# Where VectorE's expert-choice tasks stand among the steps of the attention stage: spread evenly, or by a running sum of TensorE's work

## The chip, the cores and the metric

The kernel runs on one core of a Trainium2 chip. The metric is the device time of one execution in microseconds (us); the time given for a kernel is the median of its runs. TensorE does the matrix products, VectorE reductions, comparisons and copies, ScalarE activations and copies out of the accumulator banks, GpSimd elementwise work; SyncE issues the DMAs. Each engine runs its own program in order, and they meet through semaphores.

## The reference, cut to what matters

```python
def reference(x, ctx_1024, ...):                       # x, ctx: 4 x 512 x 256
    x = x + xattn(layernorm(x), ctx_1024, ctx_1024)    # 16 heads of 16, softmax(q k^T / 4) v, Wo
    x = x + ffn(layernorm(x))
def ffn(x):                                            # product-key experts, 8 heads
    q = (rmsnorm(x) @ wq).reshape(B, T, 8, 2, 128)
    sim = einsum('bthpd,hkpd->pbthk', q, keys)         # 2 x 64 scores for each head and token
    s1, i1 = top_k(sim[0], 16);  s2, i2 = top_k(sim[1], 16)
    scores = s1[..., :, None] + s2[..., None, :]       # 256 candidates
    final_scores, pk = top_k(scores, 16)               # 16 experts of 4096
    hidden = gelu(x_norm . expert_down[idx]) * relu(final_scores)
    return sum(hidden * expert_up[idx])
```

The 2048 tokens make 16 tiles of 128. The choice of experts (both `top_k` levels) is VectorE's work.

## The kernel before

The program has two stages. In the attention stage, groups `g` = 0 to 20 (`SLOTS`) run one after the other; a group is four heads of one batch element, and has 16 steps `i`. "Step 11.9" is step 9 of group 11. At each step:

- TensorE runs the `event`s that the table `plan` gives for the step, then a turned-score product of group g - 2 (`turned_scores`), then the score product of group g (`scores`), and at every fourth step (1, 5, 9, 13) the four value products (`values`). Events: `xT`, `cT`, `proj`, `v`, `aT`, `o`, `yT` (layer norms, projections and outputs of a batch element), `max`, `oT` (each group), `down`, `wqT`, `kyT`, `wqk` (weights), `sim` (the key scores of a tile, fp32, steps 1 and 2 of even groups from 8 on), `tok` (the chosen numbers turned, step 6).
- VectorE reduces the score bank of the step to its row maxima (`tensor_reduce`, L1201), then does its other attention work if the step has any (`max_parts` at step 0, `normalise` at step 4, `first_norm` at 3 and `first_norm_apply` at 8 of groups 0, 4, 8, and in groups 6, 10, 14, 18 `residual` at steps 12 and 14 and `second_norm` at 13 and 15), and then the tasks of the choice that the table `choice` gives for the step.

TensorE may be three score products ahead of VectorE: `scores` for step n waits for the reduction of step n - 3 (`pe.wait_ge(s_max, n - 2)`, three banks). All waits are in each engine's program order, so a TensorE that waits in `scores` also holds back its events.

The choice for a tile is 17 tasks: eight `search` (a head each: top 16 of twice 64 scores, L1080 to L1092), four `choose` (two heads each, among 50 candidates a head, L1099 to L1111), one `keys` (L1120 to L1126), and four `extract` (two heads each, L1133 to L1140; the last is followed by `decode`, L1149 to L1158). Six tiles (`NA`) are chosen in this stage: tile t begins at group 8 + 2t, and its tasks stand at steps 5 to 31 counted from there, placed evenly by `spread`. The other ten tiles are chosen in the second stage.

GpSimd's program in this stage is in order too. In group g it makes, for the tile that begins there, `candidates` of heads 0 to 3 (after four searches; `choose` 0 waits for them); in the next group `candidates` of heads 4 to 7 (`choose` 2 waits for them), `expert_numbers` (`keys` waits for them), in groups 1, 5, 9 then the four `split_projection`, in groups 6, 10, 14, 18 `second_scale` twice, and last `weight_parts` after the tile's `decode`. `second_scale` is seven small instructions between VectorE's `residual` (its last instruction is L1049) and `second_norm` (L1060):

```python
                if ends:
                    candidates(tile, 1)
                    expert_numbers(tile)
                ...
                if r == 2 and b >= 1:
                    second_scale(2 * (b - 1))
                    second_scale(2 * (b - 1) + 1)
```

SyncE issues, in group g: the relay of the maxima of group g - 1, twelve loads of the score operands of group g + 1, in groups 1, 5, 9 `store_parts` four times (each after a GpSimd split), and in odd groups from 7 on the load of the next tile's input for `sim` (`load_sim_input`, L527). The second stage begins when every engine has reached `phase`; it needs the choices of tiles 0 to 5.

Of the kernel before, what the change touches and what calls it, by code (L numbers as in the profile page):

```python
# [19 lines left out]
HG = 4  # L20
NG = B * H // HG
# [45 lines left out]
def build(nc, x, ctx_in, Wq, bq, Wk, bk, Wv, bv, Wo, bo, norm_w, wq, keys, down, up, out):  # L67
    ctx = ExitStack()
    with ctx:
        def sem(name):  # L70
# [16 lines left out]
        wqk = mem.take(KD * HP * NK).rearrange("p (k n) -> p k n", k=KD)  # L87
# [4 lines left out]
        sim = mem.take(HP * NK)  # L92
# [16 lines left out]
        tok = mem.take(5 * P // 2, BF16).rearrange("p (c n) -> p c n", c=5)  # L109
# [8 lines left out]
        xT = mem.take(KD * S).rearrange("p (k t) -> p k t", k=KD)  # L118
        cT = mem.take(KD * S).rearrange("p (k t) -> p k t", k=KD)
        proj = [mem.take(S) for _ in range(2)]  # L120
# [6 lines left out]
        oT = [mem.take(S) for _ in range(2)]  # L127
        attn = mem.take(TB * D).rearrange("p (t d) -> p t d", t=TB)
        aT = mem.take(KD * S).rearrange("p (k t) -> p k t", k=KD)
# [27 lines left out]
        wqT = mem.take(2 * KD * P).rearrange("p (c k f) -> p c k f", c=2, k=KD)  # L157
        kyT = mem.take(2 * NK).rearrange("p (c n) -> p c n", c=2)
# [10 lines left out]
              for _ in range(2)]  # L169
# [10 lines left out]
        SLOTS = NG + 5  # L180
        NA = 6
        TASKS = ([("search", h) for h in range(FH)] +  [("choose", s) for s in range(4)] +
                 [("keys", 0)] + [("extract", s) for s in range(4)])

        def spread(n_tiles, first, steps):

            n = n_tiles * len(TASKS)
            return [(first + t * (steps - first) // n, t // len(TASKS), *TASKS[t % len(TASKS)]) for t in range(n)]

        def choice_start(tile):  # L190
            return 2 * HG + 2 * tile

        choice = {}
        for _t in range(NA):
            for _s, _, _kind, _i in spread(1, 5, 32):
                choice.setdefault((choice_start(_t) + _s // 16, _s % 16), []).append((_t, _kind, _i))
        before = [(0, "xT", (0, 0)), (0, "xT", (0, 1)), (0, "cT", (0, 0)), (0, "cT", (0, 1)), (0, "proj", (0, 0)),
                  (0, "proj", (0, 1)), (0, "proj", (0, 2)), (0, "proj", (0, 3)), (0, "v", (0, 0)), (0, "v", (0, 1))]
        plan = []
        for g in range(SLOTS):  # L200
            b, r = g // HG, g % HG
            ev = []
            if 1 <= g <= NG:
                ev.append((3, "max", g - 1))
            if 3 <= g < NG + 3:
                ev.append((4, "oT", g - 3))
            if r == 0 and b + 1 < B:
                ev += [(11, "xT", (b + 1, 0)), (12, "xT", (b + 1, 1)), (13, "cT", (b + 1, 0)), (14, "cT", (b + 1, 1))]
            if r == 1 and b + 1 < B:
                ev += [(2 + 3 * n, "proj", (b + 1, n)) for n in range(4)]  # L210
            if r == 2 and b + 1 < B:
                ev += [(3, "v", (b + 1, 0)), (5, "v", (b + 1, 1))]
            if r == 2 and b >= 1:
                ev += [(8, "aT", (b - 1, 0)), (9, "aT", (b - 1, 1)), (12, "o", (b - 1, 0)), (14, "o", (b - 1, 1))]
            if r == 3 and b >= 1:
                ev += [(6, "yT", (b - 1, 0)), (8, "yT", (b - 1, 1))]
            if g % 2 == 0 and g >= choice_start(0):
                tile = (g - choice_start(0)) // 2
                if tile < NA:
                    ev += [(1, "sim", (tile, 0)), (2, "sim", (tile, 1))]  # L220
                if 1 <= tile <= NA:
                    ev.append((6, "tok", tile - 1))
            if g < JL // 2:
                ev.append((7, "down", g))
            if g < HP // 2:
                ev += [(9, "wqT", g), (10, "kyT", g), (15, "wqk", g)]
            plan.append(sorted(ev, key=lambda e: e[0]))
        order = {(n, i): e for e, (_, n, i) in enumerate(before + [e for s in plan for e in s])}

        misc_full = [sem("misc_full0"), sem("misc_full1")]  # L230
# [1331 lines left out]
```

## Time and profile before

| | before |
|---|---|
| median of 3 runs | 1234.25 us (1229.91 to 1236.24) |
| the profiled execution | 1233.31 us, span 1231.5 us |
| TensorE matmuls | 1062.0 us busy, 86% of the span |
| VectorE | 948.9 us busy, 77% |
| GpSimd | 615.3 us busy, 50% |
| ScalarE | 393.8 us busy, 32% |
| mean granted TensorE clock | 0.922 |

The attention stage takes roughly the first 520 us; the part with choices in it is 214 to 516 us. Shares over the whole span mix the two stages, so the sections below go by stretches. Times of rows are us from the span's start.

### The profile page before, as it was taken

The page shows a single profiled execution, that of the slowest core. Times are in us where ns is not written, and L with a number is a line of the kernel's source. Part 1 is how long each engine was busy: PE and PEld are TensorE (multiplying, and loading weights), DVE is VectorE, ACT ScalarE, POOL GpSimd, SP SyncE. Part 2 cuts the span into 40 slices and gives each one's busy share as a digit, 9 for nine tenths or more (in the row PEclk, how much of TensorE's full clock was granted, in tenths as well). Part 3 has the DMA queues.
Part 4 walks back from the last instruction along what each step waited for, and adds up shares of the span by engine and source line. Part 5 has one row for each costly group of instructions (what it writes and reads, how often), then busy time and mean ns, then how long its engine had stood idle before and what let it go on. Part 6 is the DMA issues. An engine that isn't in the chain of part 4 may idle for free.

```text
span 1231.5 us, 28859 instructions
## 1 busy us (share of the span) xinstructions
PE 1062.0 (86%) x10152; PEld 731.2 (59%) x10152; DVE 948.9 (77%) x4836; ACT 393.8 (32%) x717; POOL 615.3 (50%) x772
## 2 busy tenths in 40 slices
PE   4899987878878777057998999999999999999998
PEld 2444443323212323036787887888878888888887
DVE  4757554968998999669899999998989989953310
ACT  2257544433444353013222222222222222222211
POOL 6320410332210313225777787877877696877511
PEclk9799998888787798556999999999999999999999
DMA  5344313221221110180010000000100010000000
GB/s 166 116 149 143 106 44 121 66 72 49 83 73 47 34 43 6 47 318 3 1 30 16 16 26 17 20 25 11 39 12 25 2 34 16 26 15 24 2 18 9
DMA packets 59924, 63.76 MB, mean 52 GB/s; under 512 B 6882, under 2 KB 56164, under 8 KB 59268
## 3 DMA queue, kind: packets, MB, share of 16 engines
q1 hardware_dynamic: 59780, 61.90, 15.7%
q8 instruction: 83, 1.36, 0.5%
q14 instruction: 61, 0.50, 0.1%
HBM read 42.21 MB, written 19.66 MB: 50 GB/s over the span
## 4 chain that ended last, share of the span: by engine, by line
PE 53%; DVE 27%; POOL 7%; issue 6%; DMA 3%; SPq 2%; ACT 2%; DVEq 0%; POOLq 0%; ACTq 0%
PE bank L1282 50%; DVE mem L1201 4%; PE bank L1285 3%; POOL mem L792 2%; DVE mem L1137 2%; DVE mem L1238 2%; DVE mem L1084 2%; DVE mem L1083 2%; SPq L492 2%; DVE mem L1088 1%; DVE mem L1133 1%; DVE mem L1140 1%; DVE mem L1080 1%; DVE mem L1092 1%; DVE mem L1120 1%
## 5 line engine op out<-in xcount | busy, mean ns | idle before, releaser
L1282 PE MATMUL bank<-mem 128*128 128x32 bf16 (+5 forms) x9672 | 1012.4, 276 | 100.2 <-DVE mem L1201 35.7
L1282 PEld LDWEIGHTS bank<-mem 128*128 128x128 bf16 (+3 forms) x9672 | 679.0, 123 | 382.9 <-issue 175.8
L792 POOL TENSOR_TENSOR mem<-mem 128x1536 bf16<-128x1536 bf16 x118 | 325.7, 2761 | 156.2 <-DVE mem L1235 151.9
L1201 DVE TENSOR_REDUCE mem<-bank 128x1 f32<-128x512 f32 x256 | 167.9, 682 | 87.1 <-PE bank L1282 86.8
L908 ACT ACTIVATE mem<-bank 128x512 f32<-128x512 f32 x256 | 149.0, 601 | 207.9 <-PE bank L1282 207.0
L1238 DVE TENSOR_TENSOR mem<-mem,bank 128x2048 bf16<-128x2048 bf16 x128 | 155.4, 1214 | 0.0
L1285 PE MATMUL bank<-mem 128*128 128x128 f32 (+3 forms) x480 | 75.9, 290 | 66.0 <-POOL mem L704 25.0
L1285 PEld LDWEIGHTS bank<-mem 128*128 128x128 f32 (+3 forms) x480 | 54.9, 142 | 113.8 <-issue 71.0
L799 POOL TENSOR_TENSOR mem<-mem 128x512 f32<-128x512 f32 x64 | 83.5, 1305 | 50.5 <-ACT mem L947 50.5
L958 ACT COPY mem<-bank 128x512 f32<-128x512 f32 x128 | 74.9, 585 | 104.8 <-PE bank L1282 104.8
L673 POOL TENSOR_TENSOR mem<-mem 128x32 f32<-128x32 f32 (+5 forms) x224 | 45.7, 242 | 117.7 <-DVE mem L1092 117.7
L1235 DVE TENSOR_TENSOR mem<-mem,bank 128x512 bf16<-128x512 bf16 x128 | 52.6, 411 | 66.0 <-PE bank L1282 56.6
L949 ACT ACTIVATE bank<-bank 128x512 f32<-128x512 f32 x64 | 37.2, 582 | 167.2 <-PE bank L1282 167.2
L947 ACT ACTIVATE mem<-bank 128x512 f32<-128x512 f32 x64 | 38.3, 598 | 163.2 <-PE bank L1282 163.2
L1252 DVE TENSOR_TENSOR mem<-bank,mem 128x512 f32<-128x512 f32 x64 | 43.8, 685 | 47.0 <-ACT bank L949 39.0
L694 POOL TENSOR_TENSOR mem<-mem 128x128 f32<-128x128 f32 x16 | 6.9, 431 | 98.9 <-DVE mem L1154 98.9
L1083 DVE FIND_INDEX8 mem<-mem 128x8 uint32<-128x64 f32 x256 | 52.9, 219 | 0.0
L1084 DVE MATCH_REPLACE8 mem<-mem 128x64 f32<-128x64 f32 x256 | 51.5, 209 | 0.0
L1137 DVE MATCH_REPLACE8 mem<-mem 128x50 f32<-128x50 f32 x256 | 46.9, 194 | 0.0
L1088 DVE MAX8 mem<-mem 128x8 f32<-128x64 f32 x256 | 44.2, 214 | 0.0
L1080 DVE MAX8 mem<-mem 128x8 f32<-128x64 f32 x256 | 43.5, 211 | 0.0
L708 POOL TENSOR_SCALAR mem<-mem 128x4 f32<-128x4 f32 x4 | 0.9, 234 | 78.2 <-DVE mem L997 78.2
(103 smaller groups left out, 764.1 us busy)
## 6 DMA issues: line engine op xcount, KB each, us to landing
mem<-parts_d SPq DMA_DIRECT2D x192, 64.0 KB, 2.3
parts_d<-mem SPq DMA_DIRECT2D x16, 384.0 KB, 2.6
mem<-in_L_ffn_expert_down SPq DMA_DIRECT2D x16, 256.0 KB, 3.0
downT_d<-mem SPq DMA_DIRECT2D x16, 256.0 KB, 3.2
mem<-downT_d SPq DMA_DIRECT2D x4, 1024.0 KB, 8.5
mem<-in_L_ffn_expert_up SPq DMA_DIRECT2D x4, 1024.0 KB, 16.7
tok_d<-mem SPq DMA_DIRECT2D x16, 160.0 KB, 1.8
mem<-tok_d SPq DMA_DIRECT2D x16, 160.0 KB, 2.4
```

Source lines behind the costliest of these rows:

```text
L792: nc.gpsimd.tensor_tensor(ow[q % 2], i0, i1, ALU.mult).then_inc(ow_rdy, 1)
L799: nc.gpsimd.tensor_tensor(gm[q % 4], gm[q % 4], coef[par][:, 2 * q:2 * q + 2, :], ALU.mult)\
L908: nc.scalar.activation(p_sb[quad % 3][:, hh, :], psum[3 + n % 2][:, :], ACT.Exp, scale=DK ** -0.5)\
L958: nc.scalar.copy(coef[1 - par][:, :, q * TK:(q + 1) * TK], src).then_inc(c_ev, 1)
L1083: steps.count(nc.vector.max_index(i[:, h, c, 0:8], s[:, h, c, 0:8], src[c]))
L1084: cut = [steps.count(nc.vector.match_replace(left[c], s[:, h, c, 0:8], src[c], GONE)) for c in range(2)]
L1088: top.append(steps.count(nc.vector.max(s[:, h, c, 8:16], left[c])))
L1137: b.append(steps.count(nc.vector.match_replace(k[:, h, :], o[:, h, 0:8], k[:, h, :], 0.0)))
L1201: nc.vector.tensor_reduce(nmx[g % 2][:, i % TB, i // TB:i // TB + 1], psum[n % 3][:, :], AX.X, ALU.max, negate=True).then_inc(s_max, 1)
L1238: nc.vector.tensor_tensor(oh[q % 2], high.to_broadcast([P, TP, P, PAIR]), numbers.unsqueeze(1).to_broadcast([P, TP, P, PAIR]), ALU.is_equa ...
L1282: return nc.tensor.matmul(o, l, r, start=first, stop=last)
L1285: return nc.tensor.transpose(o, i, ident)
```

## The change

The table `choice` is made in another way; nothing else differs. Each step gets a number, `room`: 3, and 4 for each unit of TensorE's events at the step after it (`PE_WORK`), less 4 for each unit of VectorE's own work at the step (`DVE_WORK`), and at least 1. The 17 tasks of a tile are put where the running sum of these numbers over steps 5 to 31 passes each seventeenth of its total.

```diff
-        choice = {}
-        for _t in range(NA):
-            for _s, _, _kind, _i in spread(1, 5, 32):
-                choice.setdefault((choice_start(_t) + _s // 16, _s % 16), []).append((_t, _kind, _i))
...
+        PE_WORK = {"proj": 4, "v": 5, "o": 5, "sim": 4, "xT": 2, "cT": 2, "aT": 2, "yT": 2, "oT": 2, "down": 2, "wqT": 2,
+                   "max": 1, "tok": 1, "kyT": 1, "wqk": 1}
+        DVE_WORK = {(0, 3): 4, (0, 8): 4, (2, 12): 4, (2, 13): 2, (2, 14): 4, (2, 15): 2}
+
+        def room(g, i):
+
+            own = DVE_WORK.get((g % HG, i), 0) if g < NG + HG else 0
+            after = plan[g + (i + 1) // 16] if g + (i + 1) // 16 < SLOTS else []
+            return max(1, 3 + 4 * sum(PE_WORK[name] for at, name, _ in after if at == (i + 1) % 16) - 4 * own)
+
+        choice = {}
+        for _t in range(NA):
+            _at = [(choice_start(_t) + s // 16, s % 16) for s in range(5, 32)]
+            _sum = list(itertools.accumulate(room(g, i) for g, i in _at))
+            for _n, (_kind, _i) in enumerate(TASKS):
+                _s = next(j for j, total in enumerate(_sum) if total * len(TASKS) > _n * _sum[-1])
+                choice.setdefault(_at[_s], []).append((_t, _kind, _i))
```

Worked out by the two rules, the tasks stand at these steps (s search, c choose, k keys, e extract; the group's number before the point):

```
tile 1 before: s 10.5 .6 .8 .9 .11 .12 .14 11.0 | c 11.1 .3 .4 .6 | k 11.8 | e 11.9 .11 .12 .14
tile 1 now:    s 10.5 .6 .7 .8 .9 .11 .11 .13   | c 10.13 11.1 .3 .3 | k 11.5 | e 11.6 .7 .9 .12
tile 3:        as tile 1, four groups later, before and now
tile 0 now:    s 8.5 .6 .10 .11 .12 .13 9.0 .1  | c 9.2 .3 .4 .5 | k 9.6 | e 9.7 .9 .10 .12
tile 2 now:    s 12.5 .5 .6 .7 .10 .12 .14 13.0 | c 13.2 .3 .3 .5 | k 13.6 | e 13.7 .9 .11 .13
tile 4 now:    s 16.5 .5 .7 .9 .11 .13 .15 17.0 | c 17.2 .3 .3 .5 | k 17.7 | e 17.8 .10 .12 .14
tile 5 now:    s 18.5 .6 .7 .8 .9 .11 .11 .11   | c 18.13 .13 19.1 .4 | k 19.5 | e 19.7 .7 .10 .13
before, every tile has the pattern of tile 1 before, counted from its own first group
```

The instructions of VectorE show this in two places. The first is the second half of group 10, around the first `residual` (L1040, BN_STATS and BN_AGGR) and its `second_norm` (L1060); L1080 to L1092 are one search, L1201 is the reduction of a step. Before, from step 10.12 on:

```order
L1201 TENSOR_REDUCE mem<-bank 128x1
L1040 TENSOR_TENSOR mem<-bank,mem 128x512
L1044 BN_STATS mem<-mem 128x6 x2
L1049 BN_AGGR mem<-mem 128x2 x2
L1080 MAX mem<-mem 128x8 x2
L1083 MAX_INDEX mem<-mem 128x8 x2
L1084 MATCH_REPLACE mem<-mem 128x64 x2
L1088 MAX mem<-mem 128x8 x2
L1090 MAX_INDEX mem<-mem 128x8
L1092 MAX_INDEX mem<-mem 128x8
L1201 TENSOR_REDUCE mem<-bank 128x1
L1060 TENSOR_SCALAR mem<-mem 128x256 x2
```

Now (all line numbers are 15 higher), the same steps; L1095 is the first line of a search:

```order
L1216 TENSOR_REDUCE mem<-bank 128x1
L1055 TENSOR_TENSOR mem<-bank,mem 128x512
L1059 BN_STATS mem<-mem 128x6 x2
L1064 BN_AGGR mem<-mem 128x2 x2
L1216 TENSOR_REDUCE mem<-bank 128x1
L1075 TENSOR_SCALAR mem<-mem 128x256 x2
L1095 MAX mem<-mem 128x8 x2
```

The search that stood between BN_AGGR and the `second_norm` is gone from there; the same holds for the pair at steps 14 and 15.

The second place is the end of group 11, where the tile's last task (extract and decode, L1133 to L1158) stands. Before, from the reduction of step 12 on:

```order
L1201 TENSOR_REDUCE mem<-bank 128x1
L1133 MAX mem<-mem 128x8 x4
L1137 MATCH_REPLACE mem<-mem 128x50 x4
L1140 MAX mem<-mem 128x8 x4
L1201 TENSOR_REDUCE mem<-bank 128x1 x2
L1133 MAX mem<-mem 128x8 x4
L1137 MATCH_REPLACE mem<-mem 128x50 x4
L1140 MAX mem<-mem 128x8 x4
L1149 TENSOR_SCALAR mem<-mem 128x128
```

Now, from the reductions of steps 10 to 12 on to those of steps 13 to 15:

```order
L1216 TENSOR_REDUCE mem<-bank 128x1 x3
L1148 MAX mem<-mem 128x8 x4
L1152 MATCH_REPLACE mem<-mem 128x50 x4
L1155 MAX mem<-mem 128x8 x4
L1164 TENSOR_SCALAR mem<-mem 128x128
L1166 TENSOR_SCALAR mem<-mem 128x128
L1167 TENSOR_SCALAR mem<-mem 128x128
L1169 SCALAR_TENSOR_TENSOR mem<-mem 128x128
L1172 CAST mem<-mem 128x128
L1173 CAST mem<-mem 128x128
L1216 TENSOR_REDUCE mem<-bank 128x1 x3
```

The last extract and the decode moved from behind the reduction of step 14 to behind that of step 12.

## Rows read from the trace of the kernel before

**Rows 1.** Stretches: us, busy us of PE, PEld, DVE, ACT, POOL, clock, DMA.

```profile
262.80:281.00 18.20, 16.16 (x61) 6.79 (x63) 4.06 (x8) 5.03 (x11) 1.20 (x4) 0.88 0.06 17
281.00:334.10 53.10, 42.35 (x186) 15.86 (x187) 51.03 (x304) 22.12 (x43) 11.84 (x40) 0.81 0.23 71
334.10:340.20 6.10, 5.52 (x28) 1.99 (x28) 3.27 (x8) 3.57 (x7) 0.71 (x2) 1.00 0.01 1
...
394.00:446.00 52.00, 42.37 (x184) 15.93 (x180) 50.01 (x301) 21.27 (x40) 10.94 (x38) 0.84 0.17 52
```

**Rows 2.** VectorE's waits, 281 to 334: us, times, longest.

```profile
DVE mem L1201 <- PE bank L1282: 2.4, 1, 2.4
DVE mem L1060 <- POOL mem L746: 1.6, 2, 0.8
```

**Rows 3.** TensorE's waits for reductions, 283.4 to 334: us, times, longest.

```profile
PE bank L1282 <- DVE mem L1201: 8.6, 7, 1.6
```

**Rows 4.** VectorE in order of time, steps 10.12 and 10.13: start, us.

```profile
295.69 0.30 DVE L1049 BATCH_NORM_AGGREGATE mem<-mem 128x2 f32<-128x6 f32 x2
295.90 0.32 DVE L1080 MAX8 mem<-mem 128x8 f32<-128x64 f32 x2
...
297.58 0.67 DVE L1201 TENSOR_REDUCE mem<-bank 128x1 f32<-128x512 f32 x1
299.05 0.74 DVE L1060 TENSOR_SCALAR mem<-mem 128x256 f32<-128x256 f32 x2 [0.80 <-POOL mem L746]
```

**Rows 5.** VectorE in order of time, steps 11.12 to 11.15.

```profile
326.65 0.54 DVE L1133 MAX8 mem<-mem 128x8 f32<-128x50 f32 x4
...
328.27 1.26 DVE L1201 TENSOR_REDUCE mem<-bank 128x1 f32<-128x512 f32 x2
329.46 0.53 DVE L1133 MAX8 mem<-mem 128x8 f32<-128x50 f32 x4
...
332.18 0.68 DVE L1201 TENSOR_REDUCE mem<-bank 128x1 f32<-128x512 f32 x1
```

**Rows 6.** TensorE in order of time, ends of groups 11, 13 and 15.

```profile
323.99 3.84 PE L1282 MATMUL bank<-mem 96*128 96x512 bf16 x14 [1.60 <-DVE mem L1201]
329.09 7.30 PE L1282 MATMUL bank<-mem 96*128 96x512 bf16 x21 [1.26 <-DVE mem L1201]
...
377.06 4.72 PE L1282 MATMUL bank<-mem 96*128 96x512 bf16 x14 [1.60 <-DVE mem L1201]
382.16 8.06 PE L1282 MATMUL bank<-mem 96*128 96x512 bf16 x21 [0.38 <-DVE mem L1201]
...
436.98 9.27 PE L1282 MATMUL bank<-mem 96*128 96x512 bf16 x32 [1.60 <-DVE mem L1201]
446.73 0.38 PE L1285 MATMUL bank<-mem 128*8 128x128 bf16 x4 [0.48 <-DVE mem L1018]
```

**Rows 7.** The chain that ended last, 245 to 270: start, us, what.

```profile
245.50 3.67 DMA parts_d<-mem
...
258.20 2.86 DMA mem<-xn_d
...
261.20 8.41 PE bank L1282 x19
```

**Rows 8.** VectorE and GpSimd in order of time, groups 18 and 19.

```profile
488.01 0.69 DVE L1040 TENSOR_TENSOR mem<-bank,mem 128x512 f32<-128x512 f32 x1 [0.32 <-PE bank L1282]
...
492.77 0.74 DVE L1060 TENSOR_SCALAR mem<-mem 128x256 f32<-128x256 f32 x2 [1.39 <-POOL mem L746]
...
500.51 0.13 DVE L1099 COPY mem<-mem 128x1 f32<-128x1 f32 x1
...
500.68 1.43 POOL L673 TENSOR_TENSOR mem<-mem 128x64 f32<-128x64 f32 x7 [2.55 <-DVE mem L1092]
...
502.99 0.14 DVE L1099 COPY mem<-mem 128x1 f32<-128x1 f32 x1
...
505.67 0.57 DVE L1120 SCALAR_TENSOR_TENSOR mem<-mem 128x400 f32<-128x400 f32 x1
```

More of the change, by code:

```diff
@@ L1 @@
+import itertools
 import numpy as np
```

## The prediction

> **What bounds the kernel now.** I first read the busy time by stretch. Between 281.0 and 334.1 us, which is from the first search of tile 1 (step 10.5) to step 12.0, VectorE is busy for 51.03 of 53.10 us, and in 394.0 to 446.0, the stretch of tile 3, for 50.01 of 52.00; in 262.8 to 281.0, which holds steps 10.0 to 10.4, where no task stands, it is busy for 4.06 of 18.20 us while TensorE is busy for 16.16 [rows 1]. So there are two regimes in turn: where tasks stand VectorE sets the pace, and at the first steps of every even group, where none stand and TensorE has two fp32 `sim` events, TensorE does. Next I asked what VectorE waited for. In 281 to 334 it waits once for TensorE (2.4 us, the wait that ends at 281.0, before the tile's first search) and twice for GpSimd (0.8 us each, in front of `second_norm`) [rows 2]; the other stretches with tasks before 446 us show no wait for TensorE at all inside them. TensorE on its side waits for reductions, 8.6 us in that stretch [rows 3]. That wait is the consequence of VectorE's being full, and no reserve: every microsecond of a stretch with tasks is a microsecond of VectorE's work.
>
> From this follows the point on which everything turns. The table moves work inside steps 5 to 31 of a tile; the sum of VectorE's work there stays. With no idle time in the stretch, a better fit to TensorE's events can return nothing. What can change is (a) idle time that the new order makes on VectorE, and (b) the point at which TensorE is released into the stretch that it bounds.
>
> **Part 1, the waits of `second_norm` in tiles 1 and 3.** From the end of BN_AGGR (295.69 + 0.30 = 295.99) to `second_norm` (299.05) is 3.06 us, which is GpSimd's `second_scale`; one search (295.90 to 297.58, 1.68 us) and one reduction stood in it, and 0.80 us was left as a wait [rows 4]. The new table has no task at steps 12 and 14 of groups 10 and 14. The reduction stays, the search goes, and the wait becomes 0.80 + 1.68 = 2.48 us. There are two such waits in a group: 3.4 us more of idle VectorE in tile 1, and 3.4 in tile 3. Queued behind the waiting instruction are the reductions, for which TensorE waits through the three banks, so all of it is on the path. Nothing covers it: TensorE is at most three score products ahead.
>
> **Part 2, tasks that end at an earlier step (tile 1).** The stretch that TensorE bounds begins with score product 12.0, at 329.09, released by VectorE [rows 6]; that is the reduction of step 11.13, which starts at 328.27 [rows 5]. From there TensorE runs 21 matmuls without a break, and the first search of tile 2 waits for it. Before, the last extract with the decode (329.46 to 332.18, 2.72 us) came behind this reduction and was covered by those matmuls. Now it stands at 11.12, ahead of it. The reduction comes 2.72 us later, and the work taken out of the steps before brings nothing back, because it is the same VectorE that does it earlier. Tile 1: 3.4 + 2.7 = 6.1 us. (The other way to 12.0, over score product 11.13 at 323.99, which the reduction of 11.10 releases, has two extracts of 326.65 to 328.27 = 1.62 us moved ahead of it: 3.4 + 3.2 = 6.6, less the 1.26 us that TensorE waited at 329.09. It is the shorter.)
>
> **Part 3, the same at the end of tile 2.** No `residual` stands in group 12. The last extract moves from 13.14 to 13.13, behind the same reduction as before. But an extract (1.62) moves ahead of the reduction of 13.10, which releases TensorE at 377.06, and TensorE has only 0.38 us of waiting left in front of 382.16 [rows 6]. 1.6 - 0.4 = 1.2 us.
>
> **Part 4, the end of tile 3.** Score product 15.13 (436.98) is released by the reduction of 15.10, and TensorE then runs 32 matmuls to 446.25 with the two `sim` of tile 4 in them, waits 0.48 us, and turns the maxima and group 13's output [rows 6], for which VectorE's first search of tile 4 waits. Ahead of the reduction of 15.10 come 3.4 us (part 1) and two extracts (3.2), together 6.6. Of the 0.48 us some may be absorbed; I take 6.3.
>
> **Part 5, tile 5, where VectorE alone sets the pace.** `residual` waited 0.32 and the two `second_norm` 1.39 us each (one of them in [rows 8], the other reads the same), 3.1 in all. Now all eight searches come before the first `residual`, so its 0.32 goes, no reduction is left between BN_AGGR and `second_norm`, and both wait the full 3.06 us of rows 4: 6.1, so 3.0 more. Then `choose` 2 needs `candidates` of the upper heads, which stand behind the second `second_scale` in GpSimd's program. Before, `choose` 0 and 1 (500.51 to 502.99, 2.48 us) [rows 8] covered them; now they stand earlier and only the `second_norm` itself is left as cover. `candidates` is 1.43 us (500.68) and can now start only when the second `second_scale` is over, which is when the second `second_norm` (0.74 us in rows 8) starts; with some 0.2 us of hand-over that is about 0.9 us of wait before `choose` 2. Tile 5: 3.9 us. The bounds are 3.0 (candidates hidden) and 3.0 + 2.48 = 5.5 (none of the old cover replaced).
>
> **Part 6, what I cost at nothing.** Tile 4's tasks keep their order against VectorE's other work, and no score product is left to release. Tile 0 ends earlier too (9.12 for 9.14), but the stretch after it is released elsewhere: `sim` of tile 1 starts at 261.20 when its input lands, and that load (258.20) stands in SyncE's queue behind `store_parts`, whose chain goes over the landing of the first part (issued at 245.50) [rows 7]. That store hangs on group 8's maxima and on a GpSimd split behind `candidates`. The reduction of 8.14 has six searches before it in both tables, so the maxima come at the same time; search 7 comes one reduction (0.6 us) later, and the store was not waiting for the split. The wait for the load covers up to 6 us of movement here. If the cover failed, it would cost what tile 1 pays in part 2, 2.7 us.
>
> GpSimd and VectorE do meet in tile 0. The split instructions and `keys` overlap there before and after; the row of the chain has no such delay that the new table would take away for more than about 1 us, and I count none. The Trainium skill ("SBUF — State Buffer", Terms) says of the port pair that VectorE and GpSimd share that the loser blocks for the whole instruction; by that rule `keys` at 9.6 would hold a split back by one `keys` instruction, 0.57 us by rows 8, and the sum would be 0.6 us higher at most.
>
> **The sum.** 6.1 + 1.2 + 6.3 + 3.9 = 17.5 us. The profiled execution took 1233.31, so 1250.8; the median of the runs is 0.9 above it. I say 1251, 1.4% slower.
>
> **The rivals.**
> First, only the waits count (parts 1 and 5), and TensorE's stretches start as before, because TensorE had slack there that the rows do not show: 3.4 + 3.4 + 3.9 = 10.7 us, 1245. For it: mean idle time of TensorE is large. Against it: 7.30 us without a break behind 329.09. Chance 0.17.
>
> Second, TensorE's clock. The granted clock is 0.81 in the stretch with tasks and 1.00 in the stretch after it [rows 1], and the same 21 matmuls take 7.30 us from 329.09 and 8.06 from 382.16 [rows 6], so what differs is how much of them ran at 1.2 GHz. More waiting in front could leave all three such stretches at the slower reading, or slower still: 0.8 to 1.7 us each, up to 5 more, 1256. Chance 0.14. The Trainium skill ("TensorE: Matmul & The Clock Gate", Part 1) says that the clock falls to half after TensorE has idled; it speaks against this change, and the clock columns of rows 1 agree in direction.
>
> Third, no change: the work is conserved and the new waits in front of `second_norm` are made good, because VectorE would have waited at 12.0 to 12.4 anyway. That stretch is bounded by TensorE, which is released later by the same amount, so this needs a release that does not go over VectorE. 1234 to 1237. Chance 0.08.
>
> Fourth, faster: the change does what its numbers aim at. Tasks lie under TensorE's events, and the 8.6 us of waiting of rows 3 shrink; over the four stretches of tiles 0 to 3 that would be some 30 us, and half of it gives 1219. It decides from the point at which VectorE has idle time inside a stretch to give up; by rows 2 this is 1.6 us in tile 1. Chance 0.04.
>
> My forecast has the other 0.57, and its own range is 1247 to 1255. The measurement of this kernel tells about 0.5% (6 us) from no change. Slower by more than that holds the forecast, the first two rivals, and no part of the others: 0.87 with the edges; within 0.5% 0.08, faster 0.05. The range that leaves out the last two rivals and takes in the bounds is 1241 to 1259.
>
> **What would show it.** In the changed kernel's profile: two waits of `second_norm` of about 2.5 us in group 10 and in group 14, and of 3.1 in group 18; the first search of tile 2 about 6 us later than before (340.2, the edge of rows 1), that of tile 4 13 to 14 us later, and the end of tile 5's decode 17 to 18 later; nothing before 281 us moved by more than 1 us; the second stage as long as before. Wrong would be: a first search of tile 1 that is not at 281, which breaks part 6; or a first search of tile 2 only 3.4 us late, which breaks part 2.

## The result, and the profile after

The changed kernel takes 1250.79 us (median of 4 runs, 1250.05 to 1251.22) against 1233.89 us (4 runs) before; the ratio is 1.0134, 95% interval 1.0088 to 1.0179. The profiled execution took 1250.42 us, its span is 1248.6 us.

The span by segments says more than the total. A segment ends where VectorE begins the first search of the next tile; tile 0's is cut in two at the moment when SyncE issues the load for `sim` of tile 1, and "rest" runs from the last instruction of tile 5's decode to the end. The numbers are differences of starts in the traces of the profiled executions, in us.

```
                 start  tile 0          tile 1  tile 2  tile 3  tile 4  tile 5  rest
                        to load  then
before          214.60   43.60  23.41   59.17   53.83   54.62   29.87   36.53  715.83
changed         213.64   46.07  24.00   64.22   52.77   61.69   29.87   40.46  715.84
difference       -0.96   +2.47  +0.59   +5.05   -1.06   +7.07    0.00   +3.93   +0.01
predicted            0       0      0   +6.1    +1.2    +6.3     0      +3.9    0
```

The sum came out (17.1 against 17.5), and so did tile 5, and tiles 1 and 3 to about 1 us. Two entries did not: tile 0 cost 3.1 us where nothing was forecast, and tile 2 gained 1.1 us where a loss of 1.2 was. These errors partly cancel in the sum. The forecast's own sign for part 6, a first search of tile 1 at 281, is broken: it stands at 283.7.

The stretches of the changed kernel that answer to [rows 1] (steps 10.0 to 10.4, tile 1, steps 12.0 to 12.4, tile 3); columns are the stretch, its length, busy us of PE, PEld, DVE, ACT and POOL with counts, the granted clock, the DMA share and GB/s:

```profile
264.80:283.10 18.30, 16.26 (x60) 7.52 (x63) 3.36 (x7) 5.04 (x11) 0.00 (x0) 0.86 0.11 32
283.10:339.10 56.00, 41.33 (x174) 14.93 (x174) 50.54 (x302) 21.17 (x41) 12.79 (x42) 0.76 0.20 62
339.10:347.40 8.30, 7.72 (x40) 2.48 (x38) 4.07 (x9) 4.64 (x9) 0.10 (x1) 1.00 0.00 1
400.10:461.80 61.70, 46.94 (x195) 17.40 (x191) 50.76 (x304) 23.76 (x45) 12.75 (x42) 0.78 0.14 44
```

VectorE does the same work, some 50.5 us between its first search and step 12.0, but now idles 5.5 us in it, where it was 2.1. The third row is longer than before (8.30 for 6.10) because VectorE, which has the last extract and the decode behind it by then, reaches step 12.0 sooner after TensorE does (1.8 us for 5.0), not because TensorE is slower there: from score product 12.0 to the first search of tile 2 it is 10.6 us (from 337.31), and was 11.7 (from 329.09). What VectorE waited for in tile 1, against [rows 2]:

```profile
DVE mem L1075 <- POOL mem L761: 5.0, 2, 2.5
DVE mem L1216 <- PE bank L1297: 3.2, 1, 3.2
```

(The 3.2 us are again the wait that ends before the tile's first search.) In order of time, VectorE at steps 10.12 to 10.14, against [rows 4]:

```profile
301.16 0.30 DVE L1064 BATCH_NORM_AGGREGATE mem<-mem 128x2 f32<-128x6 f32 x2
301.38 0.66 DVE L1216 TENSOR_REDUCE mem<-bank 128x1 f32<-128x512 f32 x1
304.53 0.73 DVE L1075 TENSOR_SCALAR mem<-mem 128x256 f32<-128x256 f32 x2 [2.50 <-POOL mem L761]
...
313.49 0.74 DVE L1075 TENSOR_SCALAR mem<-mem 128x256 f32<-128x256 f32 x2 [2.48 <-POOL mem L761]
```

From the end of BN_AGGR (301.46) to `second_norm` it is 3.07 us, as before; the wait went from 0.80 to 2.50. TensorE waited for reductions in the same tile as follows, 8.6 us before [rows 3]:

```profile
PE bank L1297 <- DVE mem L1216: 11.7, 8, 6.1
```

The ends of groups 11, 13 and 15 on TensorE, against [rows 6]:

```profile
332.70 10.83 PE L1297 MATMUL bank<-mem 96*128 96x512 bf16 x35 [0.92 <-DVE mem L1216]
...
385.83 6.32 PE L1297 MATMUL bank<-mem 96*128 96x512 bf16 x20 [0.92 <-DVE mem L1216]
392.56 3.73 PE L1297 MATMUL bank<-mem 96*128 96x512 bf16 x15 [0.41 <-DVE mem L1216]
...
449.74 9.67 PE L1297 MATMUL bank<-mem 96*128 96x512 bf16 x32 [1.18 <-DVE mem L1216]
459.34 0.39 PE L1300 MATMUL bank<-mem 128*8 128x128 bf16 x4
...
461.06 0.66 PE L1300 MATMUL bank<-mem 128*128 128x128 f32 x4 [1.01 <-ACT mem L897]
```

Score product 11.13, at 323.99 before, stands at 332.70, 6.6 us later when both are counted from the first search; behind it TensorE no longer waits at 12.0 but runs 35 matmuls in one piece. The 0.48 us that TensorE waited before 446.73 are gone too, but its wait for ScalarE's copy behind them grew from 0.47 to 1.01.

The chain that ended last, where tile 0 hands over to tile 1, against [rows 7]:

```profile
244.89 1.42 DVE mem L1135
246.30 0.91 DVE mem L1136
247.24 1.42 DVE mem L1139
...
249.25 0.61 DVE mem L1216
...
249.91 3.71 PE bank L1297 x6
...
254.14 0.69 ACT mem L858
...
254.88 0.62 POOL mem L734
...
259.71 2.86 DMA mem<-xn_d
...
262.70 7.35 PE bank L1297 x19
```

The chain over `store_parts` (245.50 in the kernel before) is gone; it now goes over `keys` (L1135 to L1139), a reduction, `proj(3,3)` on TensorE, ScalarE's copy, GpSimd's fourth split, and the load. And the rows of tile 5, against [rows 8]:

```profile
507.21 0.30 DVE L1064 BATCH_NORM_AGGREGATE mem<-mem 128x2 f32<-128x6 f32 x2
510.58 0.74 DVE L1075 TENSOR_SCALAR mem<-mem 128x256 f32<-128x256 f32 x2 [3.07 <-POOL mem L761]
...
518.47 0.73 DVE L1075 TENSOR_SCALAR mem<-mem 128x256 f32<-128x256 f32 x2 [3.06 <-POOL mem L761]
520.06 0.15 DVE L1114 COPY mem<-mem 128x1 f32<-128x1 f32 x1 [0.86 <-POOL mem L688]
```

Two full waits and one of 0.86 us in front of `choose` 2, as costed.

### The profile page after: what moved, and what is told of

The parts are those of the page before. It is cut to its first block, busy times and chain, and to the rows that moved or that the text cites. A ratio compares the mean times of both kernels' runs of the same rounds, so it can differ in the third digit from the quotient of the medians.

```text
span 1248.6 us, 28859 instructions
## 1 busy us (share of the span) xinstructions
PE 1065.8 (85%) x10152; PEld 733.5 (59%) x10152; DVE 950.9 (76%) x4836; ACT 394.3 (32%) x717; POOL 616.8 (49%) x772
## 3 DMA queue, kind: packets, MB, share of 16 engines
q8 instruction: 83, 1.36, 0.4%
## 4 chain that ended last, share of the span: by engine, by line
PE 52%; DVE 30%; POOL 7%; issue 6%; DMA 3%; ACT 2%; SPq 2%; DVEq 0%; POOLq 0%; ACTq 0%
PE bank L1297 49%; DVE mem L1216 4%; PE bank L1300 3%; DVE mem L1099 2%; DVE mem L1098 2%; DVE mem L1152 2%; POOL mem L807 2%; DVE mem L1253 2%; DVE mem L1103 1%; DVE mem L1095 1%; DVE mem L1155 1%; DVE mem L1148 1%; SPq L507 1%; DVE mem L1107 1%; DVE mem L1135 1%
## 5 line engine op out<-in xcount | busy, mean ns | idle before, releaser
L1300 PE MATMUL bank<-mem 128*128 128x128 f32 (+3 forms) x480 | 75.4, 288 | 72.7 <-POOL mem L719 21.8
L814 POOL TENSOR_TENSOR mem<-mem 128x512 f32<-128x512 f32 x64 | 83.7, 1308 | 50.5 <-ACT mem L962 50.5
L1095 DVE MAX8 mem<-mem 128x8 f32<-128x64 f32 x256 | 43.6, 212 | 0.0
```

The source lines that it names most:

```text
L814: nc.gpsimd.tensor_tensor(gm[q % 4], gm[q % 4], coef[par][:, 2 * q:2 * q + 2, :], ALU.mult)\
L1300: return nc.tensor.transpose(o, i, ident)
```

## The experiments

Theory: the work of VectorE is conserved, and the change costs (a) the cover of `second_norm`, (b) a later release of TensorE's stretches, and, found in the profile after, (c) the early `keys` of tile 0. Rivals: the waits are beside the path; the end costs nothing; one execution's clock made it. In all kernels here the table is written out: for each tile 17 numbers, the steps of its searches (8), choices (4), keys and extracts (4), counted from step 0 of the tile's first group. That is all that differs. The times of one kernel vary by several us from run to run, so what a single cause costs is read from the segments, of which the table below has all. Each kernel's segments come from one profiled execution. Segments with the same steps repeat within 0.3 us from kernel to kernel, apart from what the granted clock makes of them and from tile 0's way to the load.

**a1, cover back in the changed kernel.**

```diff
 tiles 1 and 3
-[5, 6, 7, 8, 9, 11, 11, 13, 13, 17, 19, 19, 21, 22, 23, 25, 28]
+[5, 6, 7, 8, 9, 11, 12, 13, 14, 17, 19, 19, 21, 22, 23, 25, 28]
 tile 5
-[5, 6, 7, 8, 9, 11, 11, 11, 13, 13, 17, 20, 21, 23, 23, 26, 29]
+[5, 6, 7, 8, 9, 11, 12, 13, 14, 16, 17, 20, 21, 23, 23, 26, 29]
```

> The changed kernel, but with work back between BN_AGGR and second_norm: in groups 10 and 14 one search moved from step 11 to 12 and choose 0 from 13 to 14; in group 18 a search at 12 and choose 0 at 14, choose 1 behind the second second_norm. Theory (idle time that the new order makes on VectorE is on the path): a search (1.68 us) and a choose (1.2) less idle in each of groups 10 and 14, and 1.7 + 1.2 + 0.9 (the wait for candidates) in group 18, 9.6 us in all: 1241, with the two waits of group 10 at 0.8 and 1.3 us. Rival (TensorE sets the pace there and the waits are beside the path): 1251, as the changed kernel.

1243.44 us (10 runs, 1238.17 to 1246.01), 1.0056 of before, interval 1.003 to 1.0082. Tiles 1, 3 and 5 are 3.2, 3.3 and 3.9 us shorter than in the changed kernel, 10.5 in all, where 9.6 were expected. In the profiled execution the start is 4.3 us and the way to the load 1.2 us longer than there, with the same steps of tile 0, so the total shows less of it. Its waits for GpSimd in tile 1 fell from 5.0 to:

```profile
DVE mem L1067 <- POOL mem L753: 2.0, 2, 1.2
```

The waits of `second_norm` are on the path.

**a2, ends back in the changed kernel.**

```diff
 tiles 1 and 3
-[..., 21, 22, 23, 25, 28]
+[..., 21, 22, 27, 28, 30]
 tile 2
-[..., 22, 23, 25, 27, 29]
+[..., 22, 23, 27, 28, 30]
```

> The changed kernel, but the last three extracts of tiles 1, 2 and 3 at steps 11, 12 and 14 as before. Theory (TensorE's stretch at the start of the next group is released later when the tasks end earlier): 2.7 + 0 to 1.2 + 3.2 us less, 1244 to 1245; the sims of tiles 2 to 4 ran wholly at 2.4 GHz in the changed kernel and partly at 1.2 before, so if they fall back up to 3 us of it is lost again, 1247. Rival (the end costs nothing, only the waits of second_norm count): 1251.

1243.93 us (10 runs), 1.0067, interval 1.004 to 1.0095. Tile 3 fell by 4.3 us against the changed kernel, tile 2 by 1.1, tile 1 by 1.65 only. In tile 1 the clock took back the rest: TensorE's stretch from 12.0 is here

```profile
334.51 7.30 PE L1289 MATMUL bank<-mem 96*128 96x512 bf16 x21 [1.69 <-DVE mem L1208]
```

the same 7.30 us as before the change, where three of its `sim` matmuls run at 1.2 GHz; in the changed kernel all but a part of the first ran at 2.4.

**a3, cover taken from the kernel before.**

```diff
 tiles 1, 3 and 5
-[5, 6, 8, 9, 11, 12, 14, 16, ...]
+[5, 6, 8, 9, 11, 11, 13, 16, ...]
```

> The kernel before, with only the searches of steps 12 and 14 of groups 10, 14 and 18 moved to 11 and 13. Theory: 3.4 us more in tile 1, 3.4 in tile 3, 3.0 in tile 5, 9.8 in all: 1243.5; nothing else moves. Rival (waits beside the path): 1234.

1245.6 us (7 runs), 1.0086, interval 1.0059 to 1.0113. Tiles 1, 3 and 5 are 3.3, 3.4 and 3.0 us longer than before, all others within 0.1: the three terms as worked out. The profiled execution took 1243.87, with a start that is 2.1 us shorter and a rest (718.81) that is 3.0 us longer than before, both in code that no table touches; where the 2 us lie by which the median exceeds the expectation is not shown.

**a4, early ends in the kernel before.**

```diff
 tiles 1 and 3
-[..., 24, 25, 27, 28, 30]
+[..., 22, 23, 24, 25, 28]
 tile 2
-[..., 24, 25, 27, 28, 30]
+[..., 22, 23, 25, 27, 29]
```

> The kernel before, with only keys and the four extracts of tiles 1, 2 and 3 moved to the earlier steps that they have in the changed kernel (last extract at 12, 13, 12). Theory: 2.7 + 1.2 + 3.2 us more, 1241; if the sims of tiles 2 to 4 then run at 2.4 GHz as they did in the changed kernel, 3.2 us come back and it is 1238. Rival (the end costs nothing): 1234, or 1231 with the clock alone.

1243.96 us (9 runs), 1.0081, interval 1.0051 to 1.0111, above the expectation. Tile 1 is 1.5 us longer, tile 2 0.3 shorter, tile 3 4.65 longer: 5.9 us where 7.1 less 3.2 for the clock were expected. In tile 1 the first four `sim` matmuls all ran at 2.4 GHz (three at 1.2 before), which is 1.2 of the 2.7 us; in tile 3 two of them ran at 1.2, where it was a part of one. The profiled execution (1241.23) again has 2.9 us more in the rest. The end of a tile at an earlier step is not free; the rival that gives it 1234 is out.

**b1 and b2, tile 0.** First all its new steps in the kernel before, then with keys and extracts put back.

```diff
 tile 0
-[5, 6, 8, 9, 11, 12, 14, 16, 17, 19, 20, 22, 24, 25, 27, 28, 30]
+[5, 6, 10, 11, 12, 13, 16, 17, 18, 19, 20, 21, 22, 23, 25, 26, 28]
...
+[5, 6, 10, 11, 12, 13, 16, 17, 18, 19, 20, 21, 24, 25, 27, 28, 30]
```

> The kernel before, with the new steps for tile 0 alone. In the changed kernel the way from tile 0's first search to tile 1's was 3.05 us longer, against 0 in the prediction. Theory (keys and the first extract now stand ahead of reduction 9.8, run while GpSimd splits, and hold back proj(3,3), behind whose split SyncE's load for sim of tile 1 stands): 3 us more here too, 1237, all of it before tile 1's first search. Rival (the 3 us were of that execution, clock or DMA): 1234.

> As b1_tile0_new, but keys and the four extracts of tile 0 at their old steps (9.8, 9.9, 9.11, 9.12, 9.14); searches and choose at the new ones. Theory: back to the way before, 0 to 0.6 us more than the kernel before, 1234. Rival (the last search, one step later at 9.1, holds back candidates and with them the splits): the 3 us stay, 1237.

b1: 1235.56 us (10 runs), 1.0008, interval 0.9984 to 1.0031; b2: 1235.87, 1.0017, 0.9997 to 1.0036. The medians can't tell 3 us here. The segment can: from tile 0's first search to the issue of the load it is 43.6 us in every kernel that has all of tile 0's old steps (before, a3, b3, c1, f1; 44.3 in a4), 47.1 in b1 and 44.6 in b2. The new steps cost 2.5 us there in the changed kernel, 3.2 in a2, 3.5 in b1 and 3.6 in a1, and between b1 and b2 the keys and extracts make 2.5 of it. b1's chain has the same links as the changed kernel's:

```profile
242.88 1.38 DVE mem L1127
244.26 0.91 DVE mem L1128
245.19 1.42 DVE mem L1131
246.63 0.86 DVE mem L1133
...
248.16 4.46 PE bank L1289 x6
```

`keys`, from its first start to its last end, takes 2.27 us in tiles 1 to 3. In tile 0 it takes 3.50 before the change, 4.37 in the changed kernel, 4.62 in b1, and 3.53 in a1, which has the new steps as well. The delay took two ways. In the changed kernel and in b1 GpSimd's fourth split waits for ScalarE's copy of `proj(3,3)`, 1.8 and 3.5 us. In a1 it does not wait; there the third split waits 4.1 us for the landing of the first `parts_d` store (1.2 before), because group 8's maxima left 2.8 us later, for which no step of tile 0 accounts. In a2 it is 3.0 us and 0.7. So b1 and b2 show the cost of early keys, and part of what a1 and a2 have there is another cause, which is open.

**b3, tile 5 alone.**

```diff
 tile 5
-[5, 6, 8, 9, 11, 12, 14, 16, 17, 19, 20, 22, 24, 25, 27, 28, 30]
+[5, 6, 7, 8, 9, 11, 11, 11, 13, 13, 17, 20, 21, 23, 23, 26, 29]
```

> The kernel before, with the new steps for tile 5 alone. Theory (both second_norm wait the whole 3.06 us, and choose 2 waits for candidates): 3.9 us more, 1238, all of it between tile 5's first search and its decode, with two waits of about 3.0 us and one of 0.9. Rival (the three moves are beside the path that ends the stage): 1234.

1241.39 us (10 runs, 1235.31 to 1244.17), 1.0057, interval 1.0028 to 1.0086. Tile 5's segment is 40.44, 3.9 longer, with the waits

```profile
DVE mem L1067 <- POOL mem L753: 6.1, 2, 3.1
DVE mem L1106 <- POOL mem L680: 0.9, 1, 0.9
```

The other 5 us of this execution stand between the load and tile 1's first search (28.32 for 23.4), where its table is that of before. They are the granted clock: its mean is 0.62 over these 28.4 us and 0.85 over the 23.5 before, and the 24 matmuls ahead of the search take 9.90 us for 5.31.

**a5, all mends together.** a1's tiles 1, 3 and 5 with a2's ends and b2's tile 0.

```diff
 tiles 1 and 3
-[5, 6, 7, 8, 9, 11, 11, 13, 13, 17, 19, 19, 21, 22, 23, 25, 28]
+[5, 6, 7, 8, 9, 11, 12, 13, 14, 17, 19, 19, 21, 22, 27, 28, 30]
```

> The changed kernel with the three mends together: work between BN_AGGR and second_norm as in a1_cover_back, last extracts of tiles 1 to 3 at their old steps as in a2_end_back, keys and extracts of tile 0 at their old steps as in b2_tile0_late_keys. The searches and choices otherwise keep the new steps. Theory (these are all the causes there are): 0 to 2 us more than the kernel before, 1235. Rival (the new steps of the searches cost something by themselves): 1239 or more.

1234.9 us (10 runs), 1.0011, interval 0.9981 to 1.0042. The expectation held; the new steps of the searches cost nothing that the interval shows. By segments they cost 1.4 us ahead of the load, and tiles 1 and 2 are 1.0 and 2.2 us shorter than before, with their `sim` at 2.4 GHz.

**c1, more cover than before.**

```diff
 tiles 1, 3 and 5
-[5, 6, 8, 9, 11, 12, 14, 16, 17, 19, ...]
+[5, 6, 8, 9, 11, 12, 12, 14, 14, 19, ...]
```

> The kernel before, with more work between BN_AGGR and second_norm than before: in groups 10, 14 and 18 two searches at step 12, the last search and choose 0 at step 14. Theory: the waits of 0.8 us in groups 10 and 14 go (1.6 us in each group), in group 18 most of 3.1 us, less some 0.5 us of waiting for candidates: 5.5 us less in all, 1228. Rival (these waits are beside the path): 1234.

1229.9 us (10 runs), 0.9966, interval 0.994 to 0.9992: faster, by less than expected. Tile 3 is 1.55 shorter (1.6 expected), tile 1 0.86, with all four `sim` of the first pair at 1.2 GHz where it was three; tile 5 is unchanged, where I had expected 2.5. The trace shows where it went. The waits of `second_norm` (2.8 us) are gone, but the two `residual` wait for TensorE, 2.9 us where it was 0.3:

```profile
DVE mem L1047 <- PE bank L1289: 2.9, 2, 2.3
```

Most of it is the clock: the same 26 matmuls between tile 5's first search and the first `residual` are 8.7 us busy at a mean granted clock of 0.54, and 6.7 at 0.64 before.

Tile 2's table is that of before, and yet it is 2.2 us shorter. So of the 4.6 us by which tiles 1 to 3 are shorter, 2.4 are the cover and 2.2 the clock. TensorE's stretch at 14.0 in c1, which answers to the 8.06 us at 382.16 in [rows 6]:

```profile
381.08 5.88 PE L1289 MATMUL bank<-mem 96*128 96x512 bf16 x21 [0.94 <-DVE mem L1208]
```

The same 21 matmuls; busy time and granted clock (third number from the end) in 382.1 to 390.2 of the kernel before are

```profile
382.10:390.20 8.10, 8.04 (x22) 2.79 (x23) 5.50 (x29) 1.55 (x4) 2.44 (x6) 0.72 0.00 0
```

and in c1 (same columns, 381.0 to 387.0)

```profile
381.00:387.00 6.00, 5.92 (x24) 2.13 (x25) 5.54 (x30) 1.30 (x3) 2.45 (x6) 1.00 0.00 0
```

**f1, f2 and f3, a better table.** f1 adds later extracts to c1, f2 three later searches in tile 0, f3 other steps for tiles 4 and 5.

```diff
 f1: tiles 1 and 2, tile 3
-[..., 24, 25, 27, 28, 30]
+[..., 24, 25, 27, 30, 33]
+[..., 24, 26, 28, 30, 33]
 f2: tile 0
-[5, 6, 8, 9, 11, 12, 14, 16, 17, ...]
+[5, 6, 8, 9, 11, 14, 16, 16, 17, ...]
 f3: tile 4, tile 5
-[..., 17, 19, 20, 22, 24, 25, 27, 28, 30]
+[..., 17, 18, 19, 19, 19, 21, 24, 27, 30]
-[5, 6, 8, ...]
+[3, 5, 8, ...]
```

> c1_more_cover, and the extracts of tiles 1 to 3 later than before: the third at step 14, the last with the decode at step 1 of the next group (where VectorE waited for TensorE), for tile 3 also the first two one step later. Theory: TensorE's stretches at 12.0, 14.0 and 16.0 are released one extract (1.6 us) earlier, up to the 2.8 and 3.6 us that VectorE has idle in them: 5 us less than c1_more_cover, 1223; if all sims of tiles 2 to 4 run at 1.2 GHz then, 1 us of it is lost. Rival (the release is not what counts): as c1_more_cover.

> f1_cover_late_end, and three searches of tile 0 moved from 8.12, 8.14 and 9.0 to 8.14 and 9.0 (two), so that group 8's maxima leave 1.6 us earlier for SyncE, behind whose queue the load for sim of tile 1 stands. Theory: the GpSimd split then gates the store, 1.1 us less than f1 before tile 1's first search, 1225. Rival (the split or the load decides anyway): as f1, 1226.

> f2_tile0, and in tile 4 the choices and keys ahead of normalise at 17.4, in tile 5 the first search ahead of normalise at 18.4. In f1 VectorE waited 2.3 and 0.9 us there for TensorE's turned output. Theory: 3 us less than f2, 1222. Rival (TensorE's and ScalarE's pace sets the end there and the wait only moves): as f2.

f1: 1225.99 us (10 runs), 0.9938, interval 0.9912 to 0.9963. Tiles 1, 2 and 3 are 2.9, 2.3 and 3.7 us shorter than before. Tiles 1 and 3 are 2.0 and 2.1 us shorter than in c1, tile 2 only 0.1; in tile 1 the `sim` of the first pair ran at 1.2 GHz for two matmuls instead of four, so about half of its gain is the clock. VectorE idles 2.1 us in tile 1's segment, 4.9 before; in 328 to 337, where it waited 2.8 us before, it waits

```profile
DVE mem L1208 <- PE bank L1289: 1.5, 3, 1.0
```

Tile 4 is 3.35 longer and tile 5 3.2 shorter than before, 66.57 against 66.40 together, with tile 4's table as before and tile 5's as in c1. VectorE waits 3.2 us in tile 4 for TensorE's turned output, which it did not before, and no longer waits in tile 5 (3.1 before). What moved the border between them I did not separate.

f2: 1223.78 us (4 runs), 0.9891, interval 0.982 to 0.9962, but from the first search to the load it has 43.60 us, f1 43.65: the 1.1 us that I expected did not come. The maxima did leave 1.4 us earlier (21.8 us after the first search for 23.2), but the first store was issued no sooner (31.1 in both), so the maxima are not what gates the load, and the lower median is not explained by it. f3: 1225.74 us (10 runs), 0.9922, 0.9889 to 0.9954. Tiles 4 and 5 together are 66.59 us, in f1 66.57: the rival held, the wait for TensorE's turned output (3.2 us in f2) only moved to ScalarE's copy:

```profile
DVE mem L1084 <- ACT mem L889: 3.4, 1, 3.4
```

All three beat both kernels; they can't be told from each other.

The segments of all kernels, as in the first table:

```
        start  to load   then  tile 1  tile 2  tile 3  tile 4  tile 5    rest
a1     217.94   47.24   23.74   60.99   52.74   58.40   29.86   36.52  716.02
a2     213.22   46.79   23.62   62.57   51.64   57.39   29.86   40.45  717.13
a3     212.53   43.62   23.48   62.46   53.78   57.99   29.85   39.49  718.81
a4     213.11   44.30   23.06   60.66   53.56   59.27   29.87   36.79  718.75
a5     214.43   44.98   23.42   58.21   51.67   54.38   29.89   36.51  715.93
b1     211.62   47.08   23.32   59.14   53.82   54.63   29.87   36.51  716.31
b2     214.93   44.56   23.49   59.37   53.93   54.66   29.86   36.55  716.11
b3     216.66   43.61   28.32   58.75   53.97   54.63   29.87   40.44  716.03
c1     214.31   43.65   23.42   58.31   51.66   53.07   29.86   36.48  719.12
f1     212.72   43.65   23.37   56.32   51.57   50.93   33.22   33.35  717.35
f2     214.08   43.60   23.43   56.37   51.59   50.93   33.23   33.34  716.86
f3     213.96   43.61   24.04   54.93   50.88   50.73   32.62   33.97  717.55
```

## Why the prediction was right, and where it was wrong

**The base.** VectorE sets the pace where tasks stand, and a table can't give back what is not idle: a5, with quite different steps of searches and choices, leaves tiles 1, 3 and 5 within 1 us of before. Right.

**Part 1** (3.4 us a tile for the cover in tiles 1 and 3): 3.3 and 3.4 in a3. a1, which puts back a search and a choice of 2.9 us together, gets back 3.2 and 3.3. Right.

**Part 2** (2.7 us for the end of tile 1): the release of score product 12.0 came 6.1 us later, counted from the first search (337.31 against 329.09, less 2.09), which is the 6.1 of the sum. But the stretch behind it was 1.1 us shorter, since its `sim` ran at 2.4 GHz. The segment shows 5.05. The step was right and the clock left out. The clock need not be the change's doing: b3, whose tile 1 has the old table, also has this stretch at 2.4 GHz.

**Part 3** (1.2 us for tile 2): the segment is 52.77, and the kernels with the old steps of tile 2 have 53.83 or, with the `sim` at 14.0 at 2.4 GHz as here, 51.66 (c1). So the later ends cost 1.1 us and the `sim` at 2.4 GHz gave 2.2. The size of the term was right, its composition only in part, and it was wrong as a forecast of the segment, sign included. The score product at 377.06 did come 1.6 us later (385.83, with 7.15 us taken off for the later first search), but 14.0 only 0.5, since the matmuls between them ended sooner at 2.4 GHz. The other 0.6 us stand one step on: score product 14.1 now waits (the 0.41 us before 392.56) for the reduction of 13.14, ahead of which the last extract and the decode have moved. I had looked at the reduction of 13.13 alone. My second rival had the clock only in the other direction: it supposed that more waiting means a slower stretch. These stretches show neither direction. TensorE's waits between tile 1's first search and the first `sim` at 12.0 add up to 14.4 us in the changed kernel and 8.2 in b3, where that `sim` ran at 2.4 GHz but for part of one matmul, and to 15.1 in a2 and 9.3 in c1, where three and four of its matmuls ran at 1.2. The rule of the Trainium skill ("TensorE: Matmul & The Clock Gate", Part 1) that I set beside it, that gaps in the work bring the clock down, does not explain that in c1 the stretch behind the longer wait is the fast one.

**Part 4** (6.3 us for tile 3): 7.07. Score product 15.13 came 6.7 us later (6.6 predicted). I had taken off 0.3 for the 0.48 us wait of [rows 6]. That wait went, but the wait for ScalarE's copy behind it grew by as much (1.01 for 0.47), and the 32 matmuls ahead took 9.67 us for 9.27, with eight small ones at 1.2 GHz where it had been four. Mis-sized by 0.8.

**Part 5** (3.9 us for tile 5): 3.93 in the changed kernel, 3.91 in b3. Right, with its three waits.

**Part 6** (tile 0 at nothing, "the wait for the load covers up to 6 us of movement here") failed: 3.1 us, of which 2.5 lie ahead of the load. The forecast had compared the new steps with the maxima, `candidates` and the first store, and had counted the meeting of `keys` with the GpSimd splits at nothing, 0.6 us at most for one blocked instruction. It had not followed the last split back to TensorE. `keys` at 9.6 now stands ahead of the reduction of 9.7 (249.17), which releases score product 9.10 and, in TensorE's order, `proj(3,3)` behind it. `keys` takes 4.37 us there beside the second split, 0.9 more than before, and `proj(3,3)` begins 36.7 us after the tile's first search instead of 32.8, and runs 3.1 us instead of 1.9, three of its four matmuls at 1.2 GHz. So the fourth split starts 1.8 us after GpSimd is free, and the last store and the load stand behind it. Moving keys and extracts back (b2) takes the wait away and 2.5 us with it; that it is `keys` and not the extracts is read from the order of the reductions and was not run by itself. 1.0 us stays with the searches and choices at the new steps. In b2 the first split starts 0.6 us later, as search 7 does, and the first store is issued 1.3 us later, since SyncE's loads ahead of it take longer; why they do is open.

So 17.1 us met the 17.5 partly by luck: 3.1 for tile 0 and 0.8 for tile 3 on one side, the clock (3.3) and an earlier start (1.0) on the other.

## What to carry to other kernels

Before weighting a layout of tasks by the partner engine's load, ask whether the engine that does them has any idle time in that stretch; if not, the only things to gain are its few waits and the moment at which the partner is released, and both ask for tasks in the middle of short dependent chains of a third engine and for ends as late as possible (f1), not for a fit step by step. When a sum of several terms meets the measurement, compare it term by term with segments of the trace: here 3.9 us of errors on one side and 4.3 on the other cancelled. Tasks that look free because a DMA is waited for may stand ahead of the event behind which that DMA is queued.

## What the runs showed of the hardware

The same TensorE instructions ran at either of two clocks, 1.2 and 2.4 GHz, in different kernels and executions. With tile 2's table unchanged, the stretch at 14.0 took 8.06 us at a mean granted clock of 0.72 in the kernel before and 5.88 at 1.00 in c1; TensorE had waited 0.38 us in front of it in the first and 0.94 in the second. In b3 the way from the load to tile 1's first search took 28.4 us at a mean of 0.62, and 23.5 at 0.85 in the kernel before, with the same instructions. What decides between the two is not shown: neither more nor less waiting in front goes with the fast stretches throughout.

VectorE's `keys` and GpSimd's split lengthen each other when they meet: `keys`, four operations that each read two SBUF tensors, took 2.27 us in tiles 1 to 3, where no split stands, and 4.37 beside one, and in the changed kernel two of the split's operations took 0.84 and 1.36 us instead of 0.61 and 1.16.

Code that no table touches varied too, the second stage with its beginning from 715.8 to 719.1 us, the part before the first choice from 211.6 to 217.9.
